# Routing of a mixture-of-experts layer: order on GpSimd, TensorE and VectorE, and where the residual sum is kept

## What is computed

```python
h = h + mha(hn, encoder_output, encoder_output, src_mask, ca_wq, ca_wk, ca_wv, ca_wo)
hn = rmsnorm(h, norm3_w)
return h + moe_ffn(hn, gate_w, exp_w1, exp_w2, sh_w1, sh_w2)

def moe_ffn(x, gate_w, exp_w1, exp_w2, sh_w1, sh_w2):
    sh = silu(x @ sh_w1.T) @ sh_w2.T                      # shared expert, all tokens
    logits = x @ gate_w.T                                  # 8 experts
    topk_vals, topk_idx = jax.lax.top_k(logits, 2)
    gates = softmax(topk_vals)                             # two chosen experts of a token
    sel = sum over the two chosen e of gate_e * (silu(x @ exp_w1[e].T) @ exp_w2[e].T)
    return sh + sel
```

## Time and profile before

| | |
|---|---|
| median of the runs | 683.35 us |
| the profiled execution: time, span | 687.49 us, 685.6 us |
| granted TensorE clock, mean share | 0.971 |
| busy: TensorE, VectorE, ScalarE, GpSimd | 590.8, 500.0, 481.9, 411.9 us |

### The profile page before, as it was taken

How to read it: one execution, slowest core, us unless ns; L and a number is a source line. 1 busy time by engine, 2 the same in 40 slices (tenths; PEclk the granted TensorE clock), 3 DMA queues, 4 the chain that set the end, 5 groups by cost and what they waited for, 6 DMA issues and landing times.

```text
span 685.6 us, 24245 instructions
## 1 busy us (share of the span) xinstructions
PE 590.8 (86%) x8126; PEld 434.6 (63%) x8126; DVE 500.0 (73%) x1210; ACT 481.9 (70%) x1355; POOL 411.9 (60%) x641
## 2 busy tenths in 40 slices
PE   6888889987888889999888867899998888888985
PEld 3556666765666656666655544699996556666664
DVE  2998999766666768888988864244432999988994
ACT  4688888776777778888866643455542787888994
POOL 5776776677777765455578876055554477764220
PEclk9999999999999999999999998999998999999997
DMA  7533433221344420101011101122225000000100
GB/s 203 143 92 88 109 81 79 67 52 41 81 117 115 115 80 25 31 24 34 25 35 40 33 29 43 33 62 68 66 67 142 25 25 25 25 18 19 38 28 28
DMA packets 49663, 42.04 MB, mean 61 GB/s; under 512 B 6409, under 2 KB 44173, under 8 KB 48544
## 3 DMA queue, kind: packets, MB, share of 16 engines
q1 hardware_dynamic: 41392, 23.13, 12.2%
q10 hardware_dynamic: 5904, 13.45, 8.3%
q0 software_dynamic: 2272, 4.24, 1.9%
HBM read 25.41 MB, written 14.79 MB: 59 GB/s over the span
## 4 chain that ended last, share of the span: by engine, by line
PE 37%; issue 26%; POOL 14%; DVE 13%; ACT 7%; DMA 2%; DVEq 1%; POOLq 1%; SPq 0%; ACTq 0%
POOL k_by_j L527 5%; PE ps L873 5%; PE ps L884 5%; PE ps L645 5%; PE ps L802 4%; DVE prob L1237 3%; PE ps L678 3%; PE ps L813 2%; DVE inv L1192 2%; PE ps L836 2%; POOL sorted_rows L550 2%; POOL rstd L509 2%; PE ps L846 2%; ACT prob_t L1017 1%; DVE stats L1312 1%
## 5 line engine op out<-in xcount | busy, mean ns | idle before, releaser
L527 POOL TENSOR_TENSOR k_by_j<-k_t,cst 128x1024 f32<-128x1024 f32 (+1 forms) x96 | 168.3, 1753 | 45.0 <-ACT k_t L962 29.2
L509 POOL TENSOR_TENSOR rstd<-spread,half_neg 128x1 f32<-128x1 f32 x80 | 44.9, 561 | 122.6 <-DVE spread L1316 72.7
L1068 ACT ACTIVATE prob<-prob 128x1024 f32<-128x1024 f32 (+1 forms) x96 | 95.0, 989 | 32.0 <-DVE prob L1237 31.5
L1225 DVE TENSOR_REDUCE top<-ps 128x16 f32<-128x1024 f32 (+1 forms) x96 | 108.2, 1127 | 9.2 <-PE ps L645 8.9
L678 PEld LDWEIGHTS ps<-cst,prob 128*128 128x128 f32 x704 | 76.7, 141 | 55.5 <-ACT prob L1068 39.4
L1192 DVE RECIPROCAL inv<-ps 128x128 f32<-128x128 f32 x96 | 91.7, 956 | 27.5 <-PE ps L813 23.5
L1237 DVE TENSOR_TENSOR prob<-ps,top 128x1024 f32<-128x1024 f32 (+1 forms) x96 | 108.2, 1127 | 0.7
L645 PE MATMUL ps<-k_by_j,q_t 64*64 64x512 f32 (+1 forms) x768 | 100.8, 596 | 0.2
L678 PE MATMUL ps<-cst,prob 128*128 128x128 f32 x704 | 96.4, 278 | 1.9 <-ACT prob L1068 1.8
L802 PE MATMUL ps<-prob_t,v 128*32 128x64 f32 x2816 | 60.8, 225 | 30.3 <-issue 13.5
L975 ACT ACTIVATE v<-ps 64x64 f32<-64x64 f32 x320 | 68.9, 215 | 19.3 <-PE ps L813 13.1
(11 more groups left out here) (163 smaller groups left out, 1234.1 us busy)
## 6 DMA issues: line engine op xcount, KB each, us to landing
sorted_rows<-zero_rows ACTq DMA_DIRECT2D x32, 276.2 KB, 2.7
stage_m<-in_m SPq DMA_DIRECT2D x80, 64.0 KB
mow<-in_mow SPq DMA_DIRECT2D x18, 256.0 KB, 3.0
stage_kv<-in_ctx_t SPq DMA_DIRECT2D x64, 64.0 KB
rows_in<-sorted_rows SPq DMA_DIRECT2D x39, 65.0 KB
x_t<-in_x_t SPq DMA_DIRECT2D x16, 64.0 KB, 1.9
stage_kv<-in_x_t SPq DMA_DIRECT2D x16, 64.0 KB
stage_kv<-x_t SPq DMA_DIRECT2D x16, 64.0 KB
```

The lines of the kernel that those rows point to most:

```text
L527: pool.tensor_tensor(k_by_j[:, p, 0:nj, :], k_t[:, p:p + 1, :].broadcast_to([128, nj, TOK]), cst[:, cj:cj + nj].unsqueeze(2).broadcast_to( ...
L1068: act.activation(prob[:, p, 0:w], prob[:, p, 0:w], ACT.Exp, scale=float(D // heads(pr)) ** -0.5).then_inc(exp_d, 1)
L1225: dve.tensor_reduce(top[:, p, 0:nh].rearrange("p (b h) -> p b h", b=2), sc, AX.X, ALU.max).then_inc(top_d, 1)
```

## The change

Four edits, and the counting that goes with them:

1. GpSimd: `chosen` and `taken` (pair s-7) move from behind `k_by_j` to the front of the phase-3 slot, ahead of the copy of rows, the root and the keys.
2. TensorE: the rank product (pair s-8) moves from behind the transposes to ahead of them, directly behind the scores.
3. VectorE: `rank` moves from behind the subtraction to ahead of the maximum.
4. Phase 3's sum is written by VectorE into `x_tok` directly (`kept(pr)`), instead of into `y`; `squares` and ScalarE's normalisation read it there, and GpSimd's copy of line 499 is left out in phase 3 (16 copies of 128x128). The copies of phase 2 stay. `res_d` no longer counts phase 3; those who waited for it there wait for `y_d` or not at all.

```diff
+        def wait_res(eng, pair, back=0):
+            n = RES_BEFORE[pair.phase] + pair.i - back + 1
+            if not (isinstance(n, int) and n <= 0):
+                eng.wait_ge(res_d, n)
+        def kept(pair):
+            return x_tok[:, pair.i, :] if pair.phase == RO else y[:, pair.p, :]
...
@@ gpsimd, ahead of the step at(OFF_XT); taken out again behind k_by_j
+                pr = follows(at, OFF_R2, RO)
+                if pr is not None:
+                    p, i = pr.p, pr.i
+                    wait_own(pool, r_h, pr)
+                    wait_own(pool, r_p, pr, 2)
+                    pool.tensor_tensor(chosen[:, p, :], hot[:, i, 0, :], hot[:, i, 1, :], ALU.add).then_inc(r_c, 1)
+                    wait_own(pool, r_c, pr)
+                    wait_own(pool, r_t, pr, 1)
+                    pool.tensor_tensor(taken[:, i + 1, :], taken[:, i, :], chosen[:, p, :], ALU.add).then_inc(r_t, 1)
...
                 elif pr is not None and POST[pr.phase] == "rms":
-                    wait_pair(pool, y_d, pr, 0, apart=True)
-                    pool.tensor_copy(x_tok[:, pr.i, :], y[:, pr.p, :]).then_inc(res_d, 1)
                     if pr.phase == RO:
                         wait_pair(pool, norm_d, pr)
                         pool.tensor_copy(token_rows[:, pr.i, 1, 0:D], token_rows[:, pr.i, 0, 0:D]).then_inc(r_two, 1)
+                    else:
+                        wait_pair(pool, y_d, pr, 0, apart=True)
+                        pool.tensor_copy(x_tok[:, pr.i, :], y[:, pr.p, :]).then_inc(res_d, 1)
...
@@ tensor: the step at OFF_PV with the transposes now stands behind the step at OFF_RP
@@ vector, ahead of at(OFF_SCORE) with top; taken out again behind prob
+                pr = follows(at, OFF_RP, RO)
+                if pr is not None:
+                    wait_own(dve, r_p, pr)
+                    wait_own(dve, r_m, pr, 2)
+                    dve.tensor_tensor(rank[:, pr.p, :], ps[:, B_F, 256:256 + E], base, ALU.add).then_inc(r_k, 1)
...
@@ scalar
-                        wait_pair(act, res_d, pr, 2)
+                        if pr.phase == FF + 1:
+                            wait_res(act, pr, 2)
                         wait_pair(act, rstd_d, pr)
-                        act.activation(row_buffer(pr), y[:, p, :], ACT.Copy, scale=rstd[:, p, :]).then_inc(norm_d, 1)
+                        act.activation(row_buffer(pr), kept(pr), ACT.Copy, scale=rstd[:, p, :]).then_inc(norm_d, 1)
@@ vector
-                    if not (isinstance(pr.n, int) and pr.n < 2) and POST[ph] != "none":
-                        wait_pair(dve, res_d, pr, 2)
-                    dve.tensor_tensor(y[:, p, :], ps[:, B_OUT, OUT], x_tok[:, pr.i, :], ALU.add).then_inc(y_d, 1)
+                    if POST[ph] != "none" and ph != RO:
+                        wait_res(dve, pr, 2)
+                    dve.tensor_tensor(kept(pr), ps[:, B_OUT, OUT], x_tok[:, pr.i, :], ALU.add).then_inc(y_d, 1)
...
-                dve.wait_ge(res_d, RES_BEFORE[RO] + SUB * (t + 1))
+                dve.wait_ge(y_d, RO * NP + SUB * (t + 1))
...
-RES_BEFORE = [NP * sum(k != "none" for k in POST[:n]) for n in range(len(POST))]
+RES_BEFORE = [NP * sum(k != "none" for m, k in enumerate(POST[:n]) if m != RO) for n in range(len(POST))]
```

More of the change, by code:

```diff
@@ L491, in slot @@
                     wait_pair(pool, norm_d, pr)
-                    if not (isinstance(pr.n, int) and pr.n == 0):
-                        pool.wait_ge(res_d, pr.n)
+                    wait_res(pool, pr, 1)
                     pool.tensor_tensor(scaled[:, p, :], normed[:, p, :], g, ALU.mult).then_inc(gsc_d, 1)
@@ L529, in slot @@
                         .then_inc(kj_d, 1)
[L531 to L539, removed]
                 pr = follows(at, OFF_RS, RO)
@@ L669, in slot @@
                         .then_inc(l_acc, 1)
[L671 to L680, removed]
                 pr = follows(at, OFF_RP, RO)
@@ L693, in slot @@
                         .then_inc(r_p, 1)
+                pr = at(OFF_PV)
+                if pr is not None:
+                    p, npr = pr.p, heads(pr) // 2
+                    wait_pair(pe, exp_d, pr)
+                    for half, done in enumerate((pt0_d, pt1_d)):
+                        for k in range(npr // 2):
+                            q = half * (npr // 2) + k
+                            mm = pe.transpose(ps[:, 2 * p + half, k * 128:(k + 1) * 128],
+                                              prob[:, p, q * 128:(q + 1) * 128], ident)
+                        mm.then_inc(done, 1)
                 pr = at(OFF_V)
@@ L1091, in slot @@
                     if POST[pr.phase] == "rms":
[L1092 removed]
+                        if pr.phase == FF + 1:
+                            wait_res(act, pr, 2)
                         wait_pair(act, rstd_d, pr)
[L1094 removed]
+                        act.activation(row_buffer(pr), kept(pr), ACT.Copy, scale=rstd[:, p, :]).then_inc(norm_d, 1)
                     else:
[L1096 removed]
+                        act.wait_ge(res_d, RES_BEFORE[LAST] - 1 if isinstance(pr.i, int) and pr.i == 0 else RES_BEFORE[LAST])
                         wait_pair(act, y_d, pr)
@@ L1209, in slot @@
                     wait_own(dve, f_nn, pr, 2)
-                    wait_pair(dve, res_d, pr)
+                    wait_res(dve, pr)
                     dve.tensor_tensor(y_f[:, p, :], ps[:, B_F, 0:D], x_tok[:, pr.i, :], ALU.add).then_inc(f_y, 1)
@@ L1243, in slot @@
                 one, two, three = follows(at, OFF_R1, RO), follows(at, OFF_R2, RO), follows(at, OFF_RP, RO)
-                if three is not None:
-                    r = three.p
-                    wait_own(dve, r_p, three)
-                    wait_own(dve, r_m, three, 2)
-                    dve.tensor_tensor(rank[:, r, :], ps[:, B_F, 256:256 + E], base, ALU.add).then_inc(r_k, 1)
                 if two is not None:
@@ L1256, in slot @@
                 if three is not None:
+                    r = three.p
                     wait_own(dve, r_k, three)
@@ L1318, in slot @@
                         wait_pair(dve, y_d, pr)
-                        dve.tensor_tensor_reduce(squares[:, p, :], y[:, p, :], y[:, p, :], 1.0 / D, EPS,
+                        dve.tensor_tensor_reduce(squares[:, p, :], kept(pr), kept(pr), 1.0 / D, EPS,
                                                  ALU.mult, ALU.add, spread[:, p, :]).then_inc(spread_d, 1)
```

3 lines of the change are left out of this document (1 added, 2 removed).

## The result

The changed kernel takes 676.32 us (median of 4 runs, 675.77 to 677.81), beside 684.2 us for the kernel before on the same chip: a ratio of 0.988 [0.986, 0.991], 7.9 us faster. A second series gave 0.9885 [0.985, 0.993].

What follows compares the result with a forecast made beforehand. The prediction took two nearly equal loops, GpSimd and VectorE with TensorE, to bound the kernel. Savings of 1.0 (slots 53 to 57), 1.8 (slots 58 to 63) and 1.1 us (drain) made 3.9: 683.35 to 679.4 us, range 676.5 to 682.6.

Steps and rivals of the forecast that it cites:

- What bounds the kernel: Phase-3 slots: two loops of nearly equal length, GpSimd at 6.3 to 6.4 us, VectorE with TensorE beside it.
- The second loop: VectorE with TensorE: 5.74 us a slot plus waits for `chosen` and `rank` and a 0.41 us TensorE standstill.
- Slots 58 to 63: Slot falls from 6.45 to 6.15 us (5.74 + 0.41), saving 1.8 us; ends 0 and 2.7.
- if the idle 0.55 stays behind the keys: GpSimd ahead of the first scatter: 0.55 us idle time assumed to remain, giving 0.20 us saved a slot.
- Carry-over of the profile: Savings summed on a profiled execution of 687.49 us, 4.1 above the median 683.35, applied to the median unscaled.
- Slots 53 to 57: VectorE's 0.37 us wait in slot 57 goes and the first scatter comes earlier: 1.0 us; ends 0.4 and 1.2.
- Drain: From the root of slot 65 to `chosen` of slot 68: 1.1 us saved; ends 0.5 and 2.2.
- Edits with one answer: Rank product and `rank` moves add no instruction; without cover 0.2 us a slot, 2.4 us over 12 slots.
- Everything loosens: Rival, chance 0.15: all upper ends reached in the slots and the drain, gain 6.1 us, time 677.2 us.
- The other loop decides: Rival, chance 0.17: TensorE's standstill grows or moves, slot stays near 6.4 us, gain 1.6 us, time 681.7.
- The gain is given back: Rival, chance 0.10: shared expert begins no sooner or loses the gain on TensorE's clock; time 683 us.
- Slower: Rival, chance 0.08: GpSimd's keys meet VectorE's small steps, about 1 us in each of 7 slots; 686.5 us.

Runs made afterwards that it cites:

- part 1 alone: Kernel before with only GpSimd's `chosen` and `taken` moved to the front of the slot: 679.57 us, ratio 0.994.
- part 4 alone: Kernel before with only phase 3's sum written to `x_tok` directly and GpSimd's 16 copies gone: 681.53 us, ratio 0.997.
- no_rank: Changed kernel with TensorE's rank product and VectorE's `rank` put back behind transposes and subtraction: 680.61 us, ratio 0.993.
- the second profile: The kernel before, unchanged, profiled once more: 685.71 us, ratio 1.0006.
- only_rank: Kernel before with only the rank product moved ahead of the transposes and `rank` ahead of the maximum: 694.89 us, ratio 1.0165.
- taken_behind_keys: Changed kernel with `taken` moved between keys and scatter, `chosen` staying at the slot's front: 677.19 us, ratio 0.988.

## Why the prediction was right and where it failed

**What bounds the kernel: half right.** GpSimd full was right, and it is the whole answer for slots 58 to 63: part 1 alone took 0.26 us off the slot, part 4 alone 0.21, all parts 0.56, each what GpSimd's own spacings say. The second loop "at 5.74 plus what those waits and the stall add" was wrong in both of its terms.

**Slots 58 to 63, 1.8 us forecast, 4.0 measured.** The step that failed is "5.74 + 0.41 = 6.15 us". The 5.74 was taken from inverse to inverse as VectorE's own work, without reading the rows between; 0.34 us of it was the wait for the logits, and parts 2 and 3 together take 0.41 away (no_rank 5.72, changed 5.31). The same paragraph says that TensorE's logits no longer stand behind VectorE's subtraction, and then subtracts nothing for it. The 0.41 is a standstill of one execution, which no other profile has in this stage. With 5.31 VectorE decides nothing, and GpSimd's figure of 6.1 should have stood, less the second error: "if the idle 0.55 stays behind the keys". It became 0.18 us, which is 0.37 a slot, 2.2 us in six slots. The upper end of 2.7 us allowed for 6.0 us a slot only; the slot is 5.71.

**Carry-over of the profile.** The sum was made against an execution 4.1 us slower than the median, and carried over "without scaling". Its stage was 106.5 us where the second profile has 104.2; against the first the stage fell by 10.0 us, against the second by 7.75, and the medians by 7.9. A stall without releaser in a slow execution was the thing to distrust.

**Slots 53 to 57, 1.0 forecast, 1.3 measured.** The 0.37 us of VectorE's wait went, as said. What it left out are the logits: slot 56 went from 6.16 to 5.31 us, slot 57 from 5.75 to 5.31.

**Drain, 1.1 forecast, 2.5 measured** (3.2 with the second profile of the changed kernel). From the root of slot 65 to `chosen` of slot 68 the gain is 1.5 us, from 13.10 to 11.59, and 2.3 with that second profile (10.84), against the forecast 1.3. The forecast kept 0.55 us idle ahead of these scatters too; 0.20 or 0.36 are left. Up to that root the forecast let VectorE's gain end, and 1.0 us more came. It is VectorE's own, since the root waits for it both before and after. This is the root of slot 65 in the second profile of the kernel before:

```profile
396.73 0.57 POOL L509 TENSOR_TENSOR rstd<-spread,half_neg 128x1 f32<-128x1 f32 x1 [0.92 <-DVE spread L1319]
```

VectorE's slot 64 fell from 5.76 to 5.25 us, and its slot 65 up to `spread` from 5.83 to 5.36: the same slip, the wait for the logits counted as work. "The root of 67 can become late on VectorE, about 0.2 us" came true in one of two profiles (0.23 us; none in the other).

**Edits with one answer.** That the product behind the scores "adds no instruction" and costs 0.2 us a slot without its cover was six times too small: only_rank shows 1.2 us a slot (7.50 beside 6.27), since the cover was not the scores but `chosen` being early. The condition stood in the text ("`chosen` comes about 3 us sooner and is asked for about 1.1 us sooner"), but its price was not worked out. It is the largest number of this case: part 1 is what makes parts 2 and 3 safe. That the sum in `x_tok` costs nothing on VectorE held (5.70 beside 5.75).

**The rivals.** "Everything loosens" came nearest (677.2), though it loosened for other reasons than those given. "The other loop decides" fell with the 5.31. "The gain is given back": the forecast "same 4.4 us" behind `chosen` was 5.33 in one profile and 4.37 in the other, and the last scatter kept its distance in both. The granted clock that spoke for this rival, 1.00 and 0.87, was 0.85 and 0.93 in the same two stretches of the second profile before, and 0.85 and 0.94 in the changed kernel. "Slower" did not come. The Trainium skill ("SBUF — State Buffer", section "SBUF: two separate sides") has the loser of the shared port pair blocked for the whole instruction; where `chosen` meets VectorE's squares in the changed kernel it takes 0.24 to 0.25 us (0.33 once) in the place of 0.19 to 0.22. Where the copy of the rows runs beside the squares there, these take 0.35 to 0.38 us instead of 0.29. They start 0.06 to 0.08 us behind that copy of 0.29 us, so by these rows a full block would cost them an estimated 0.2 us; the traces show 0.06 to 0.09, and the measurement decides. What stretches the squares to 0.41 to 0.48 us in six slots of the second profile before, where GpSimd's copy starts only 0.37 to 0.44 us behind them, is open.

**The idle time ahead of the scatter.** The Trainium skill ("Perfetto Trace Analysis", section "DMA Instruction — SWDGE (GPSIMD)") has the sequencer push an instruction that waits into a wait queue and be ready for the next one at once. If the waits here fall under that rule, a wait of `taken` would leave the scatter's preparation covered. The trace disagrees: 0.18 us idle without that wait, 0.55 with it, and the measurement decides. The kernel writes its waits as statements of their own, and `taken` has two or three; whether each of them waits in that queue, no run shows.

## What to carry to other kernels

Before a slot's length is called an engine's own work, read its rows one by one for a wait in the middle; and before a stall without a releaser enters a sum, look whether a second execution has it. An operation placed behind a wait is only as early as what is waited for: ask for the whole ring, from the waiting instruction through the other engines back to it, and price it with the other edits absent. Where GpSimd is full as here, put independent work between two operations of which the second waits for the first, and, ahead of an indirect DMA, work behind the one that waited: the keys cover the 0.74 us, a short copy covers a part. And before a run is read as a test of a wait, count which result the wait is for.

## What the runs showed of the hardware that was not expected

- On GpSimd, an operation that waits for the one directly ahead starts 0.27 to 0.33 us after that one's start instead of 0.15 (`chosen`), or 0.36 instead of 0.26 (behind the 128x128 copy), and an indirect DMA right behind it has 0.55 us idle ahead of it instead of 0.18. With a copy between, the DMA still starts 0.74 us behind the start of the operation that waited.
- TensorE stood still for 0.24 to 0.44 us, with no releaser, inside eight products of one execution and in this stage never in the profiles of the others. It ended 1.3 to 1.4 us behind a scatter's start each time; why is open.
- VectorE's slot 57 is 5.31 us in the changed kernel and 5.25 in all those where GpSimd's `taken` or copy stands elsewhere or is gone. The step that holds the 0.06 us is `squares`: 0.35 us where GpSimd's copy of the rows runs beside it, 0.29 in taken_behind_keys, where that copy ends at 346.64 and `squares` starts at 346.70. In slots 55 to 57 of the changed kernel it is so each time; slot 57:

```profile
345.06 0.29 POOL L519 COPY token_rows<-token_rows 128x128 f32<-128x128 f32 x1
345.14 0.35 DVE L1332 CUSTOM_DVE_ANT_0 squares<-x_tok 128x128 f32<-128x128 f32 x1
```
